# The last 16 relation types of a graph layer packed for two edge tiles as row tiles of 64 partitions, with their types from an int16 transfer

## The reference, cut to what matters

```python
m = x[src] * rel[edge_type]              # 106,250 edges, 400 relation types, 256 features
m = concatenate([m[:half] @ W_in, m[half:] @ W_out])
agg = segment_sum(m * norm[dst], dst)    # edges are sorted by dst
h = tanh(agg + x @ W_loop + b)
```

## Time and profile before

| | |
|---|---|
| median of three runs | 3587.01 us |
| the profiled execution | 3595.48 us, its span 3593.7 us |
| edge stage of layer 0 | about 99 to 1486 us |
| edge stage of layer 1 | about 1639 to 3024 us |
| busy: PE, DVE, ACT, POOL | 84%, 66%, 52%, 54% |
| granted TensorE clock, mean | 0.917 |

### The profile page before, as it was taken

One profiled execution on the slowest core, in us unless ns is written; L12 is line 12 of the kernel. 1 busy time (PEld: TensorE's weight loads), 2 busy tenths in 40 slices (PEclk: granted clock), 3 DMA queues, 4 the chain that ended last, 5 costly groups with the idle time before them and its releaser, 6 DMA issues. The chain is left out here.

```text
span 3593.7 us, 61044 instructions
## 1 busy us (share of the span) xinstructions
PE 3030.8 (84%) x21236; PEld 2804.9 (78%) x21236; DVE 2375.1 (66%) x3620; ACT 1851.9 (52%) x3333; POOL 1927.0 (54%) x2028
## 2 busy tenths in 40 slices
PE   3788888888888888796988888888888887776998
PEld 1688888888788888696887777788887786776998
DVE  5566666666666666794666666666666666996666
ACT  5455555555555555484555555555555554444443
POOL 3655555555555555355555555555555553774332
PEclk9898999899989898897899999988999988998999
DMA  7222222222222222243222222222222222332222
GB/s 233 86 80 82 80 80 83 79 81 79 81 81 79 81 81 80 70 163 95 78 81 81 81 81 81 81 79 80 80 80 81 81 81 70 109 114 91 71 70 67
DMA packets 163452, 313.57 MB, mean 87 GB/s; under 512 B 34381, under 2 KB 96269, under 8 KB 163189
## 3 DMA queue, kind: packets, MB, share of 16 engines
q0 software_dynamic: 79872, 218.21, 21.1%
q1 hardware_dynamic: 82389, 91.10, 7.9%
q10 hardware_dynamic: 928, 0.85, 0.1%
HBM read 264.16 MB, written 45.88 MB: 86 GB/s over the span
## 5 line engine op out<-in xcount | busy, mean ns | idle before, releaser
L606 PE MATMUL edge_rg<-edge_rel_hi,edge_hot 128*128 128x256 f32 x6656 | 1654.7, 306 | 93.4 <-issue 76.7
L606 PE MATMUL edge_rg<-edge_rel_lo,edge_hot 128*128 128x256 f32 x4992 | 1405.4, 305 | 42.6 <-issue 40.7
L606 PEld LDWEIGHTS edge_rg<-edge_rel_hi,edge_hot 128*128 128x128 f32 x6656 | 1321.5, 213 | 137.6 <-issue 129.6
L450 ACT ACTIVATE edge_hot<-edge_typ,minus_type 128x512 fp32r<-128x512 f32 x832 | 527.1, 685 | 1331.1 <-PE edge_typ L595 648.4
L606 PEld LDWEIGHTS edge_rg<-edge_rel_lo,edge_hot 128*128 128x128 f32 x4992 | 1066.0, 214 | 87.3 <-issue 72.5
L424 POOL DMA_INDIRECT edge_xg<-h,src x832 | 787.5, 947 | 591.1 <-DVE edge_rg L502 354.8
L424 POOL DMA_INDIRECT edge_xg<-emb,src x832 | 788.7, 948 | 586.3 <-DVE edge_rg L502 338.9
L502 DVE TENSOR_TENSOR edge_rg<-edge_xg,edge_rg 128x1024 f32<-128x1024 f32 x416 | 509.7, 1225 | 678.7 <-remote 569.1
L493 DVE TENSOR_SCALAR edge_hot<-edge_typ,type_of 128x512 fp32r<-128x512 f32 x832 | 584.5, 743 | 184.7 <-ACT edge_hot L450 117.2
L508 DVE TENSOR_TENSOR edge_m_lo<-edge_rg,edge_m_hi 128x1024 fp32r<-128x1024 f32 x416 | 504.1, 1212 | 2.3 <-ACT edge_m_hi L442 2.3
L456 ACT ACTIVATE edge_hot<-edge_hot 128x512 fp32r<-128x512 f32 x832 | 484.0, 639 | 0.0
(11 more groups left out here) (160 smaller groups left out, 3946.9 us busy)
## 6 DMA issues: line engine op xcount, KB each, us to landing
edge_xg<-emb,src POOLq DMA_INDIRECT x832
edge_xg<-h,src POOLq DMA_INDIRECT x832
set_x_rows<-in_x SPq DMA_DIRECT2D x25, 256.0 KB, 3.7
emb<-set_e_rows SPq DMA_DIRECT2D x25, 256.0 KB, 3.5
emb_t<-set_e_t SPq DMA_DIRECT2D x25, 256.0 KB, 3.0
dense_prev<-emb_t SPq DMA_DIRECT2D x25, 256.0 KB, 2.8
h_t<-dense_work SPq DMA_DIRECT2D x25, 256.0 KB, 2.0
h<-dense_work SPq DMA_DIRECT2D x25, 256.0 KB, 2.2
```

Of the source, the lines that this page charges most:

```text
L450: act.activation(hot[:, q % 2, c], typ[q % 2][:], ACT.Abs, bias=K["minus_type"][:, c:c + 1]).then_inc(distances, 1)
L606: ins = pe.matmul(rg[q % 2][:, t, :], hot[:, q % 2, c, t * P:(t + 1) * P], part[:, c, :], start=(c == 0 and part is rel_hi), stop=(c == FULL))
```

## The change

In both edge stages the fourth chunk (the last 16 types) gets a form of its own:

- It is no longer one chunk of 128 partitions per tile. Two tiles share one chunk: partitions 0 to 63 (strip 0) hold tiles 0 and 1 of a group, partitions 64 to 127 (strip 1) tiles 2 and 3. In a strip, 16 rows are the high parts, 16 the low parts, and 32 match no type. The one-hot rows are `hot_rest`, 128 x 256 per group in place of 128 x 512.
- PE makes its product with the rest first: for tiles (0, 2), then for (1, 3), two matmuls that read 64 partitions each, one from each strip, into different halves of `rg`. There are still 28 matmuls per group.
- DVE builds `hot_rest` not from `typ` in PSUM but from int16 types in SBUF. `phase_setup` casts the types to int16 and ACT stores them to DRAM (two DMAs); in the edge stages SP loads 128 x 512 of them for every two groups, spread over the 64 partitions of a strip (104 loads per layer, two buffers, `rest_in`). DVE waits for `rest_in` before `hot_rest`.
- At the start of an edge stage, eight loads of the last 16 relation rows replace a memset and two loads, and two masks `is_low`, `is_high` put the high and low parts in place (three DVE operations over 128 partitions for one over 16).

```diff
@@ phase_setup
+            dve.tensor_copy(types_h[0:TYPE_ROWS], types_i[0:TYPE_ROWS]).then_inc(types_cast, 1)
...
+            act.wait_ge(types_cast, 1)
+            for t in range(STRIPS):
+                act.dma_start(types_16[ds(t, 1)].rearrange("o (r k) -> r (o k)", r=TYPE_ROWS)
+                              .rearrange("r (h e) -> r h e", h=2),
+                              types_h[0:TYPE_ROWS].rearrange("r (h t e) -> r h t e", h=2, t=STRIPS)[:, :, t, :])\
+                   .then_inc(types_out, 16)
@@ phase_edges
+            def load(g, q, i):
+                if q % 2 == 0:
+                    wait_past(sp, hot_done, g + 2 - GROUPS_IN_RING)
+                    sp.dma_start(rest[:, q // 2].rearrange("p a e -> p (a e)"),
+                                 types[:, ds(g * PART, 2 * PART)].unsqueeze(1).to_broadcast([STRIPS, STRIP, 2 * PART]))\
+                      .then_inc(rest_in[q // 2], 16)
...
-            act.wait_ge(rel_zero, 1)
-            for at in (0, 32):
+            for at in range(0, P, REST):
                 act.dma_start(rel_sb[at:at + REST, FULL, :], rel[FULL * P:RELS, :]).then_inc(rel_in, 16)
...
-                for c in range(HOT_ACT, RCHUNKS):
-                    ins = dve.tensor_scalar(hot[:, q % 2, c], typ[q % 2][:], K["type_of"][:, c:c + 1], None,
-                                            ALU.is_equal)
-                ins.then_inc(hot_done, 1)
+                for c in range(HOT_ACT, FULL):
+                    dve.tensor_scalar(hot[:, q % 2, c], typ[q % 2][:], K["type_of"][:, c:c + 1], None, ALU.is_equal)
+                dve.wait_ge(rest_in[q // 2], 16 * (i + 1))
+                dve.tensor_scalar(hot_rest[:, q % 2], rest[:, q // 2, q % 2], K["type_of"][:, FULL:], None,
+                                  ALU.is_equal).then_inc(hot_done, 1)
...
-                for t in range(GROUP):
-                    for c in range(RCHUNKS):
-                        for part in (rel_hi, rel_lo) if c < FULL else (rel_hi,):
-                            ins = pe.matmul(rg[q % 2][:, t, :], hot[:, q % 2, c, t * P:(t + 1) * P], part[:, c, :],
-                                            start=(c == 0 and part is rel_hi), stop=(c == FULL))
+                for tiles in ((0, 2), (1, 3)):
+                    for h, t in enumerate(tiles):
+                        strip = slice(h * STRIP, (h + 1) * STRIP)
+                        pe.matmul(rg[q % 2][:, t, :], hot_rest[strip, q % 2, t % 2 * P:(t % 2 + 1) * P],
+                                  rel_hi[strip, FULL, :], start=True, stop=False)
+                    for t in tiles:
+                        for c in range(FULL):
+                            for part in (rel_hi, rel_lo):
+                                ins = pe.matmul(rg[q % 2][:, t, :], hot[:, q % 2, c, t * P:(t + 1) * P], part[:, c, :],
+                                                start=False, stop=(c == FULL - 1 and part is rel_lo))
```

More of the change, by code:

```diff
@@ L22 @@
 I32 = mybir.dt.int32
+I16 = mybir.dt.int16
 U32 = mybir.dt.uint32
@@ L54 @@
 RCHUNKS = FULL + 1
-assert 0 < REST and 2 * REST <= P
+STRIPS = 2
+STRIP = P // STRIPS
+PART = GROUP * P // STRIPS
+assert 0 < 2 * REST <= 32 and REST & REST - 1 == 0
 HID = 512
@@ L149, in phase_setup @@
         types_i = s.sb("types_i", [P, 2 * GROUP * P], I32)
+        types_h = s.sb("types_h", [P, 2 * GROUP * P], I16)
+        rows = s.sb("rows", [P, 4], I32)
+        no_type = s.sb("no_type", [P, 1])
         real = s.sb("real", [P, TILES])
@@ L217, in _ @@
             pool.memset(K["minus_half"][:], -0.5).then_inc(consts, 1)
+            pool.iota(rows[:, 0:1], [[0, 1]], base=0, channel_multiplier=1).then_inc(consts, 1)
             pool.memset(K["eps"][:], EPS).then_inc(consts, 1)
@@ L294, in _ @@
             dve.tensor_copy(K["span"][:], span_max[:]).then_inc(chain, 1)
[L296 to L298 removed]
+            dve.tensor_scalar(rows[:, 1:2], rows[:, 0:1], REST - 1, None, ALU.bitwise_and).then_inc(chain, 1)
+            dve.tensor_scalar(rows[:, 2:3], rows[:, 0:1], REST, None, ALU.bitwise_and).then_inc(chain, 1)
+            dve.tensor_scalar(rows[:, 3:4], rows[:, 0:1], 2 * REST, None, ALU.bitwise_and).then_inc(chain, 1)
+            dve.wait_ge(chain, 16)
+            dve.tensor_scalar(no_type[:], rows[:, 3:4], float(RELS), float(FULL * P), ALU.mult, ALU.add).then_inc(chain, 1)
+            dve.wait_ge(chain, 17)
+            dve.tensor_tensor(K["type_of"][:, FULL:], rows[:, 1:2], no_type[:], ALU.add).then_inc(chain, 1)
+            dve.tensor_scalar(K["is_low"][:], rows[:, 2:3], 1.0 / REST, None, ALU.mult).then_inc(chain, 1)
+            dve.tensor_scalar(K["is_high"][:], rows[:, 2:3], 0.0, None, ALU.is_equal).then_inc(chain, 1)
+            dve.wait_ge(chain, 20)
             dve.tensor_scalar(K["minus_type"][:], K["type_of"][:], -1.0, None, ALU.mult).then_inc(chain, 1)
@@ L355, in over_groups, with phase_edges @@
         turn(STEPS + t // GROUPS_IN_RING, t % GROUPS_IN_RING)
-def phase_edges(nc, K, layer, nodes, rel):
+def phase_edges(nc, K, layer, nodes, rel, types):
     first = layer == 0
@@ L370, in phase_edges @@
         pick = s.sb("pick", [P, P], F32R)
-        hot = s.sb("hot", [P, 2, RCHUNKS, GROUP * P], F32R)
+        rest = s.sb("rest", [P, GROUPS_IN_RING // 2, 2, PART], I16)
+        hot = s.sb("hot", [P, 2, FULL, GROUP * P], F32R)
+        hot_rest = s.sb("hot_rest", [P, 2, PART], F32R)
         xg = s.sb("xg", [P, RING, DIM])
@@ L384, in phase_edges @@
         sums_t = [v[:, 512 - (DC + 1) * WIN:].rearrange("p (k n) -> p k n", n=WIN) for v in small]
-        rel_zero = s.sem("rel_zero")
         rel_in = s.sem("rel_in")
         rel_split = s.sem("rel_split")
+        rest_in = [s.sem(f"rest_in{b}") for b in range(2)]
         picked = s.sem("picked")
@@ L412, in phase_edges, with _ @@
         block = ctx.enter_context(nc.Block())
+        @block.sync
+        def _(sp):
+            def load(g, q, i):
[4 more added lines that the diff above has]
+                      .then_inc(rest_in[q // 2], 16)
+            over_groups(sp, (0, load))
         @block.gpsimd
@@ L1398, in build @@
         keep("minus_type", [P, RCHUNKS])
+        keep("is_low", [P, 1])
+        keep("is_high", [P, 1])
         keep("minus_half", [P, 2])
```

40 lines of the change are left out of this document (23 added, 17 removed).

## The result

The changed kernel takes 3634.52 us (median of 4 runs, 3629.89 to 3639.76), the kernel before 3586.43 us beside it: ratio 1.0134, 95% interval 1.0115 to 1.0154. That is 48 us slower where no change was forecast; it lies inside the range, and in the 0.33 given to slower. The profiled execution of the changed kernel took 3639.76 us, its span is 3638.0 us. Unless it says otherwise, what follows compares the two profiled executions.

The account below looks back on a forecast made before the run. Taken as bound: a loop of message, POOL's eight gathers and a late matmul completion, 6.57 us per group. Terms -5 + 0 + 0 + 3 + 0.7 = -1 us gave 3586 us, no change; range 3530 to 3650.

Parts of the forecast that it names:

- the 0.33 given to slower: Whole kernel: chance 0.33 that the change makes it slower, from rivals B and C.
- The loop itself: Edge stages: message 1.23, POOL's start 0.27, eight gathers 9.70, late release 1.94; 13.14 us per two groups.
- PE, per group: Edge stages: two pairs replace four matmul slots; 0.08 us more per group, bounds 0.24 less to 0.32 more.
- Neither engine's work passes on to the time: Edge stages: PE and DVE work is hidden, since both layers run at the same pitch to 0.005 us.
- SP's loads: Edge stages: loads of types have some 13 us to land; taken 0, upper bound +92 us.
- Start: Start of each edge stage: eight small loads replace two; 1.5 us per layer, +3 us together, bounds 0 and +8.
- setup: Setup: a cast on DVE ahead of its chain, up to +0.7 us.
- DVE: Edge stages: a shorter operation builds the one-hot rows; saves 0.45 us per group; with PE on the path, -5 us.
- Rival C: Edge stages: changes of shape stop PE, so the second message misses POOL's fourth gather; 3711 us, chance 0.06.
- B: Edge stages: the new DVE operation slows POOL's gathers; 3641 to 3708 us, chance 0.28.
- A: Edge stages: PE sets the pace, two slots saved per group; -112 us, 3475 us, half of that 3530; chance 0.27.
- D: Edge stages: the pairs do not run side by side; PE 0.32 us more per group, hidden, time as forecast.

Follow-up runs that it names:

- Runs 2: Kernel before with each tile's first matmul issued twice (four more full matmuls per group), on the chip where that kernel takes 2931.47 us: 3132.85 us, ratio 1.069.
- 9: Kernel before with each tile's first matmul issued twice (four more full matmuls per group), on a chip that holds completions: 3691.76 us, ratio 1.0282.
- run 8: Changed kernel with full matmuls over 128 partitions in place of the pairs, loads kept, on a chip that holds completions: 3600.68 us, ratio 1.0043.
- run 10: Changed kernel, pairs kept, with SP's loads of types left out after the first four groups: 3594.96 us, ratio 1.0024.
- run 11: Changed kernel with SP's first load of types held back until the relation rows have landed: 3622.71 us, ratio 1.0084.
- run 5: Kernel before, unchanged, profiled on another chip, where completions were held: 3521.58 us.
- run 1: Changed kernel with full matmuls in place of the pairs, on the chip where the kernel before takes 2931.47 us: 2942.24 us, ratio 1.0037.

## Why the prediction was wrong

- **The loop itself** was read rightly: eight gathers, the held completion, the message are there after as before, and POOL's idle time of 3.61 us at 424.11 shows it. That the held completions belong to POOL's gathers stays argued from the traces; no run took the gathers off POOL.
- **"PE, per group", 0.08 us more, bounds to 0.32: the step was mis-sized.** It measured 0.52. The two strips run side by side, as assumed, but the row for the change of shape (0.20 us from L622 to L630) showed only the way there; the way back costs 0.19 (0.31 from the pair to the first full matmul, less a slot), and the full matmul behind it 0.10 more. The Trainium skill (TensorEngine Tiling (Array Packing), Key Properties) says that a change of mode drains TensorE and that tiles run in parallel; by both the trace agrees (0.50 us a pair; the x2 rows).
- **"Neither engine's work passes on to the time" failed for PE.** It rested on layers 0 and 1 having one pitch in spite of 0.08 us of PE. That test was too small for the conclusion. Runs 2 and 9 put it plainly: +0.48 us on PE cost 0.48 us per group where nothing is held, and 0.25 where completions are; and with the loads present the pairs cost 34 us (3634.52 against run 8's 3600.68, ratios 1.0134 and 1.0043). Without the loads they cost 8 at most (run 10), so "hidden" held there. What hides PE's time in a run of eight is, as the timelines show it, the distance of the second message's end from the end of POOL's fourth gather. The prediction had both numbers, 416.55 and 417.4 us, a margin of 0.85 us, from one loop. In the changed kernel's loop shown above 0.37 us is left (415.12 to 415.49). Many loops never had it: 40 of 118 runs were fours before the change. There the second message waits for PE (1.51 us before the one at 409.30), and their period grew most, by 0.35 us.
- **"SP's loads, taken 0, upper bound +92": wrong.** Removing them alone takes 33 to 39 us (1.0115 to 1.0134 down to 1.0024) off the changed kernel, and adding loads of half the bytes alone costs the kernel before 17. The reason given for 0 (they have 13 us to land) is true, no DVE operation waited for them (DVE was idle 0.0 us before L537), and it does not matter: the loop gets longer by their being there. By which step it does, no run shows.
- **"Start, +3", bounds to 8, and setup, +0.7:** together 7.2 us, all in layer 0, mis-sized; the term left out that SP's loads go ahead of the relation rows (4.0 us, run 11).
- **DVE, 0.45 us saved:** 0.743 became 0.351 us, so 0.39 saved, worth nothing that could be told, as forecast (-5).
- **Rival C** comes nearest: PE's idle time before L649 is 32.7 us, runs of four became the rule in layer 0 (68 of 132), and "a loop broken in two keeps its sum" held. Its mechanism (stops of PE) was not the one; the batch is simply longer. **B** is excluded by the gathers' mean: in the trace of the changed kernel 394 gathers ran beside the new operation, and their median is 0.946 us like that of the other 1270. So the rule of the Trainium skill (SBUF — State Buffer, "two separate sides") made no price here; whether the new operation is of the kind that it speaks of, no run shows. **A** had PE's time on the path in full, and slots saved, which PE's time does not show. The 0.52 us that PE gained would then be 0.52 x 416 = +216 us, and it was 48, and run 9 paid half. So it is wrong on the chips that hold completions; on the first one PE does set the pace. **D** is excluded by the x2 rows.

**Open:** why the loads and the pairs together cost more than their sum; what of a load costs when its packets are spread or gone; and why 32 full matmuls (run 9, +104 us) cost so much more than 24 full ones and two visits without loads (run 10, +8 us), though PE's shortest turn in layer 0 is about the same in both, 5.53 and 5.56 us. The rhythm of layer 1, which run 9 does not find, cannot be all of it: in layer 0, where neither is in the rhythm, the two stand 43 us apart as well (1416.1 and 1372.8).

## What to carry to other kernels

Equal pace in two stages shows only that the small difference between them is hidden: look for the deadline that hides it, and compare the margin in front of it with what the change adds, in all loops and not in one (here 0.85 us in the loop that was read, and none in 40 of 118). A matmul pair of half height costs its two changes of shape (0.50 us here against 0.24 for the two full slots it replaces, and 0.63 against 0.48 for two pairs in one visit), so pack only what fills a longer visit than these, and put what shares the shape beside it only if its inputs are ready then. A transfer that nobody waits for need not be free: here 17 us by itself, and 33 to 39 beside the pairs.

## What was not expected of the hardware

One program took 2931 us in one group of runs and 3522 to 3593 us in the others. What goes with it is whether completions reach the other engines late while POOL issues gathers. Where they do, 50 to 67% of PE's completions in the edge stages stand over 0.3 us behind the end of their matmul, and 9 to 41% of ACT's and DVE's, so it is not the matmuls' alone. These shares are rough, since some records of completions are missing; in layer 0 of run 5 those of the relation rows are whole, and half of them came late, by up to 4.9 us. In run 1 it is at most 6% in any 100 us, and in the stages between and behind the edge stages it is none, in any trace. DVE waited 807.9 against 12.2 us for its messages. What is worth doing depends on it: the change with one visit for both pairs cost 2.4% on the first chip, and the whole change costs 1.2 to 1.3% on the others.
